# Two weight reads on 12 and on 4 DMA engines behind the first spread reads of images 2 and 3

## What is computed

```python
# x: [4, 64, 16, 16]
x = x + deformable_conv(layernorm_over_channels(x))
t = tokens(x)                                  # [4, 256, 64]
t = t + mixture_of_experts(layernorm(t))
# deformable_conv: a 3x3 convolution gives, per pixel and tap k of 9, an offset (dy, dx) and a mask
#   sampled[c, k, p] = mask * bilinear(x[c], y + ky + dy, x + kx + dx)   (0 outside the image)
#   out[o, p] = sum over c, k of w_dcn[o, c, k] * sampled[c, k, p]
# mixture_of_experts: 8 experts, the two best by a gate, weighted by a softmax of their logits
#   out = sum over e of weight[e] * (gelu(x @ W1[e] + b1[e]) @ W2[e] + b2[e])     64 -> 256 -> 64
```

## Time and profile before

| what | value |
|---|---|
| median of 3 runs | 97.97 us (96.95, 97.97, 98.33) |
| the profiled execution: span from the first to the last instruction | 95.2 us |
| the profiled execution's own time | given by its span alone; the runs lie 1.75 to 3.13 us above that span |
| PE busy | 85.9 us, 90% |
| DVE busy | 67.5 us, 71% |
| ACT busy | 45.1 us, 47% |
| POOL busy | 22.9 us, 24% |
| transfers | 10.02 MB, mean 105 GB/s over the span |
| granted TensorE clock | 1.000 |

### The profile page before, as it was taken

The page is one execution under the profiler, slowest core; times in us unless marked ns, Lnnn a source line. Parts: engine busy times, 40 slices in busy tenths (PEclk is TensorE's granted clock), DMA queues, the critical chain, the costliest instruction groups (busy, mean ns, idle before and its releaser), DMA issues.

```text
span 95.2 us, 1718 instructions
## 1 busy us (share of the span) xinstructions
PE 85.9 (90%) x574; PEld 46.9 (49%) x574; DVE 67.5 (71%) x185; ACT 45.1 (47%) x88; POOL 22.9 (24%) x33
## 2 busy tenths in 40 slices
PE   3986899899888998989999899999899999999980
PEld 3973356559545974556463544344342332223550
DVE  5695999898899997895955965957936820069550
ACT  5113575969050632341275765418462769652200
POOL 5204000000000072997200002002553150005630
DMA  1719600000419999983999994000000000000003
GB/s 47 213 30 284 267 0 3 0 7 0 121 36 274 262 253 260 260 271 112 249 257 253 251 260 123 0 0 0 3 7 0 0 0 0 0 0 0 0 7 103
DMA packets 5303, 10.02 MB, mean 105 GB/s; under 512 B 1344, under 2 KB 2400, under 8 KB 5296
## 3 DMA queue, kind: packets, MB, share of 16 engines
q1 hardware_dynamic: 4960, 9.54, 37.5%
q0 software_dynamic: 192, 0.30, 1.0%
q10 hardware_dynamic: 144, 0.10, 0.3%
HBM read 9.08 MB, written 0.85 MB: 104 GB/s over the span
## 4 chain that ended last, share of the span: by engine, by line
PE 34%; DMA 21%; DVE 17%; issue 14%; POOL 6%; SPq 3%; POOLq 1%; ACT 1%; DVEq 0%; ACTq 0%
DMA spread_hats<-hat_rows 10%; DMA hat_rows<-hrow_last 8%; PE taps_ps L791 6%; PE bank_o L882 6%; PE hid_ps L869 6%; POOL rs L326 4%; PE bank_o L817 3%; PE taps_ps L869 3%; DMA xt<-in_x_tok 2%; PE bank_c L760 2%; DVE xn L619 2%; PE bank_y L882 2%; SPq L312 2%; DVE a_sb L547 2%; DVE at L535 2%
## 5 line engine op out<-in xcount | busy, mean ns | idle before, releaser
L817 PE MATMUL bank_o<-a_sb,v_sb 128*64 128x256 f32 x144 | 18.0, 386 | 1.0 <-ACT a_sb L412 0.5
L454 ACT ACTIVATE hid<-hid_ps,b_col 128x512 f32<-128x512 f32 x18 | 11.5, 683 | 10.2 <-PE hid_ps L869 10.1
L817 PEld LDWEIGHTS bank_o<-a_sb,v_sb 128*64 128x64 f32 x144 | 9.7, 136 | 8.3 <-issue 2.3
L547 DVE TENSOR_TENSOR a_sb<-spread_hats 128x1536 f32<-128x1536 f32 x6 | 10.9, 1834 | 2.9 <-DMA spread_hats<-hat_rows 2.9
L791 PE MATMUL taps_ps<-ident,at 128*128 128x128 f32 x72 | 11.0, 280 | 1.5 <-DVE a_sb L669 0.8
L326 POOL TENSOR_TENSOR rs<-ve,power 128x2 f32<-128x2 f32 (+1 forms) x6 | 4.8, 806 | 25.7 <-DVE ve L562 21.5
L412 ACT ACTIVATE a_sb<-taps_ps 128x512 f32<-128x512 f32 x11 | 6.4, 597 | 9.2 <-PE taps_ps L791 9.2
L869 PE MATMUL hid_ps<-x2s,w_sb 64*128 64x512 f32 x36 | 10.2, 641 | 0.0
L791 PEld LDWEIGHTS taps_ps<-ident,at 128*128 128x128 f32 x72 | 7.9, 141 | 4.6 <-DVE a_sb L669 3.3
L882 PE MATMUL bank_o<-hid,w_sb 128*64 128x512 f32 x40 | 9.7, 605 | 0.0
L454 ACT ACTIVATE hid<-taps_ps,b_col 128x512 f32<-128x512 f32 x14 | 8.8, 686 | 1.5 <-PE taps_ps L869 1.5
(11 more groups left out here) (133 smaller groups left out, 121.3 us busy)
## 6 DMA issues: line engine op xcount, KB each, us to landing
spread_hats<-hat_rows SPq DMA_DIRECT2D x18, 384.0 KB, 8.1
w_sb<-in_w SPq DMA_DIRECT2D x2, 512.0 KB, 3.9
wdcn<-in_w_dcn SPq DMA_DIRECT2D x2, 144.0 KB, 3.0
xc<-in_x_ch SPq DMA_DIRECT2D x1, 256.0 KB, 4.5
hat_rows<-hrow SPq DMA_DIRECT2D x2, 128.0 KB
hat_rows<-hrow POOLq DMA_DIRECT2D x2, 128.0 KB, 8.1
xt<-in_x_tok SPq DMA_DIRECT2D x1, 192.0 KB, 2.4
out<-xc SPq DMA_DIRECT2D x1, 128.0 KB, 1.7
```

The source lines that it names most:

```text
L454: act.activation(hid[:, m % H_RING, half, c, :], two_banks(f"H{h}.{j}.{c}")[:, half * 512:(half + 1) * 512], ACT.Gelu, bias=b1_col[:, col: ...
L547: dve.tensor_tensor(a_sb[:, slot % A_RING:slot % A_RING + GROUP, :, :], spread_hats[:, 1:, k0:k0 + GROUP, :].rearrange("p s k t -> p k s t ...
L817: last = pe.matmul(bank_o[st * O:(st + 1) * O, 0:HW], v_sb[:, img, st, k, :], a_sb[:, slot % A_RING, st, :], start=(k == 0), stop=(k == TA ...
```

## The change

Behind the three spread reads of the first unit of image 2 and of image 3, SyncE issues two more reads. The first takes 12 rows of a view of the weight `w2` in HBM, each 12 KB long, into 12 neighbouring partitions of `tmp` (from partition 0 for image 2, from 64 for image 3), the second 4 such rows into four partitions that begin 32 further on. The data is not used: `tmp` is overwritten by its steps. Every `tmp` step waits until all four of these reads have landed (semaphore `skewed`, 64). The other engines' lists are as before; the line numbers grow by 2 to 8.

```diff
+SKEW, SKEW_RUN = (12, 4), 4 * GROUP * HW
...
+        skewed = sem("skewed")
...
                     for s in range(ST):
                         down = flat[0, s * RPT:(s + 1) * RPT].unsqueeze(0).broadcast_to(shape)
                         sp.dma_start(spread_hats[:, 1 + s, taps, :], down).then_inc(there, 16)
+                    if g == 0:
+                        for n, engines in enumerate(SKEW):
+                            first = 64 * i + 32 * n
+                            sp.dma_start(tmp[first:first + engines, :, :, :].rearrange("p h j t -> p (h j t)")[:, 0:SKEW_RUN],
+                                         w2.rearrange("(a b) e c o -> a (b e c o)", b=4)[0:engines, 0:SKEW_RUN]).then_inc(skewed, 16)
...
                     dve.wait_ge(y_done, upto("O" + step[3:]))
                     dve.wait_ge(*saved(spread_saved, f"ss{h}.{j // 2}"))
+                    dve.wait_ge(skewed, 16 * len(SKEW) * (NB - DIRECT))
```

## The result

The changed kernel takes 102.37 us (median of four executions, 100.89 to 103.88) against 97.88 us for the kernel before beside it. The ratio is 1.034 with a 95% interval of 1.022 to 1.046: slower, and inside the predicted range. This ratio is made from the two executions in which TensorE kept its full clock, 100.89 and 101.23 us; in the other two its mean granted clock was 0.966 and 0.967, and they took 103.50 and 103.88 us. The profile is one of the first kind, with a span of 99.1 us where the kernel before had 95.2. What the other kind is comes with the last experiment.

A forecast was written before the change was run, and what follows sets the result against it. The prediction took a nearly full, in-order TensorE from 43 us on as the bound. It added 0.6 us (image 2) and 2.58 us (unit 10), 3.2 us in all, to the 97.97 us median: 101.2 us, range 97.0 to 103.2 us.

The forecast's parts named there:

- The bound: From 43 to 90 us TensorE is nearly full: earlier data gains at most 1.0 us, later data adds to the end.
- The extra bytes: The extra reads between an image's first and second unit: 3.46 us, as four engines filling four neighbouring partitions share one entrance.
- The later pace: Spread reads behind the extra ones: 1.25 us each, between 0.96 and 1.54, as the shift separates some engine pairs, not others.
- Unit 10: Image 3's second product: its reads need 7.21 us after unit 9 instead of 4.63, 2.58 us late (+1.33 to +3.84).
- Each sign named for it: Behind unit 9: rate well under 255 GB/s, engines busy, 2 us or more idle before unit 10's product, TensorE idle as much.
- Image 2: Its later reads delay the write of image 3's hat rows, and everything of image 3, by 0.6 us (0 to 1.7).
- Not at the edge: Image 2's products have slack: their accumulations stand behind other steps, and VectorE idles 1.18 us before a step behind the second.
- SyncE's issues: Four more issues of about 0.6 us push those of units 7 and 10 back by 1.2 us, at no cost.
- VectorE's new wait: Before nine steps, the first at 65.83 us: never waits; one more semaphore check costs between 0 and 0.04 us.
- dear by bytes alone: Rival, chance 0.22: the extra reads cost only their bytes, the later pace stays; 99.7 us.
- the shift works: Rival, chance 0.20: extra bytes cost 0.96 us, later reads 0.96 us each; TensorE gives back 0.7 us; 97.3 us.
- Different engines: Rival, chance 0.04: the two reads use 12 and the other 4 engines, nothing shifts, unit 10 0.5 to 0.8 us late; 98.8 us.

The follow-up runs named there:

- the last experiment: The changed kernel measured again, unedited, beside the kernel before: 102.30 us (101.10 to 104.23, six executions), ratio 1.051 (1.042 to 1.061).
- the twelve-run measurement: Second measurement, on twelve executions, of the changed kernel with its extra reads into partitions eight apart: ratio 1.001 (0.996 to 1.007) to the kernel before.
- the repeat: The changed kernel measured again, unedited, beside the kernel before: 102.30 us, ratio 1.051 (1.042 to 1.061); its profile is an execution at 0.966 clock.
- the reads eight apart: The changed kernel with its extra reads into partitions eight apart, not neighbouring: ratio to the kernel before 0.987 on four executions, 1.001 on twelve.
- the lone reads: The kernel before plus four early reads, each four engines with 16 KB, awaited singly: 4.37, 2.84, 2.88, 3.23 us into partitions 1, 4, 8, 32 apart.

## Why the prediction was right

**The bound held.** TensorE full from 43 us on, late data straight to the end, earlier data worth little: the loss of 3.3 us is idle time of TensorE, and the kernels with early data gained nothing that the twelve-run measurement can tell.

**The extra bytes** were to cost 3.46 us through one entrance. The trace's completion marks put the last extra read 2.75 us after unit 9 (54.96 against 52.21), 3.00 us in the repeat: the mechanism, crowding by the place that is written, is right, shown by the reads eight apart, the packets and the lone reads, and the size is 0.5 to 0.7 us too large. What was wrong is the place: the text put the extra reads strictly behind unit 9, but their packets begin at 49.30 us, 2.9 us before unit 9 lands, so unit 9 may pay a part, as worked out under its name below. By the last marks alone the split between these reads and those behind them is rough.

**The later pace** of 1.25 us per read was a middle between two ends. The three reads of unit 10 took 59.12 - 54.96 = 4.16 us, 1.39 each, those of unit 11 3.51 us, 1.17 each: 1.28 over the six, 1.14 in the repeat. By the same marks it was 1.46 us before ((59.70 - 50.97) / 6), and not 1.54. The reason given for it, pairs a half block apart, is the step that the runs do not bear out; which engine fills which partitions no view here shows.

**Unit 10** was to come 7.21 us after unit 9 and came 6.91 us (6.84 us in the repeat), so it was delayed by 2.11 us instead of 2.58 us. Each sign named for it was there: under 255 GB/s with busy engines, 2.83 us of idle time before the product, 2.16 us before the accumulation.

**Image 2** was to add 0.6 us. The hat rows came 0.72 us later, as thought, and the run with image 2 alone measured +0.5 us (0.1 to 1.0). Two details of the working do not hold: the 2.5 us of the earlier trace rows that it takes for image 2's write is the wait for image 3's rows (image 2's lasted 2.0 us, 24.79 to 26.81), and the two writes go through different queues, so that the 5.3 us are not shown to be the wait behind image 2's reads.

**Unit 9, without a term.** It came 1.25 us later, 0.5 us more than the hat rows. Image 2's reads are not shown to do this: with image 2 alone unit 9 is on time. The nearer cause is image 3's own extra reads, which start before unit 9 has landed. From the issue of its first read to its landing unit 9 took 8.37 us (43.84 to 52.21), where it took 7.85 us before. In the four profiles of kernels whose extra reads of image 3 go into neighbours it took 8.07 to 8.52 us, in the ten others 6.78 to 7.85 us. Image 3 alone has 8.07 us with neighbours and 6.78 us eight apart. These are single profiles, so the cause is supported and not shown. On the chain 0.72 + 0.52 + 2.11 = 3.35 us stand against the forecast 0.6 + 2.58 = 3.18 us. What unit 10 was late by less than forecast, unit 9 was late by more: image 3's part is 2.63 us where 2.58 us were forecast. The closeness is in part luck, since single profiles scatter here by more than these differences.

**"Not at the edge"** was wrong for image 2's products. Unit 7's came 2.46 us later (42.97 against 40.51), VectorE normalised later, and TensorE waited 1.07 us at the transposes of line 839. It seems to have cost nothing of its own, since TensorE would have waited as much more for unit 9; the repeat, which lacks this wait, waits 1.29 us there instead of 0.55 us. With image 2 alone unit 7's product is 1.25 us late (41.76) and this wait is not there.

**Without a term: the clock.** The sum gives 101.2 us, and the three executions at full clock took 100.89 to 101.23 us. The median of the first four is 1.2 us higher because two of them also lost 2.6 us to the slow clock (103.69 against 101.06 us on average); of all ten, seven lost some. The text looked at the granted clock, found it full, and asked what late data costs in idle time, but not what a new idle time may do to the clock behind it. That the median lies inside the range owes something to luck and to a wide range: four of the ten executions, 103.50 to 104.23 us, lie above its upper end of 103.2 us, a figure for which the text gives no working.

**The rest.** SyncE's issues were hidden, VectorE's new wait never held. Of the rivals, *dear by bytes alone* is excluded by the reads eight apart; *the shift works* describes those kernels rightly in that crowding decides, but its 0.7 us did not show in the twelve executions. *Different engines* was not tested by an edit, but the packets speak against it: in the repeat, four of the sixteen 12 KB packets of image 3 begin 0.001 to 0.002 us after another of them has ended (50.020 and 50.022, 50.625 and 50.626, 50.912 and 50.914, 51.094 and 51.096), which fits two packets one behind the other on one engine.

## What to carry to other kernels

Before adding a small read beside a busy stream, ask where in the on-chip memory it lands: four engines that fill four neighbouring partitions at once were slower than four that fill partitions four or eight apart, and everything behind them in the queue waits. Where TensorE is full and works in order, price a late transfer by the idle time that it makes, and then ask whether that idle time may bring the clock down, which went with nearly as much again here. A gain of one per cent on four executions should be measured again before it is believed.

## What the runs showed that was not expected

- TensorE's clock fell to half for 6.8 us after waits of 1.29 and 2.08 us in a stretch that was otherwise full, and stayed at full after waits of 1.07, 0.55 and 2.16 us in another execution of the same kernel.
- A lone read of four times 16 KB took 4.37 us into neighbours, 2.84 us into partitions four apart and 3.23 us into partitions 32 apart.
- Unit 9's reads took 8.07 to 8.52 us where the extra reads behind them in the queue go into neighbours, and 6.78 to 7.85 us elsewhere.
- With some of the extra reads ahead of them the spread reads of image 2 ran at 282 to 375 GB/s and not at 252 GB/s, with others not (244 GB/s with eight engines); the cause is open.
- The issue of the last two stores took 1.06 to 1.77 us in five profiles and 0.82 to 0.84 us in the other nine; the cause is open.
